# Cross-attention: where the first-pass matmuls of a block stand among its second-pass pairs

## What is computed

```python
q = qp.reshape(bsz, t, H, D).transpose(0, 2, 1, 3)      # H = 16, D = 32, t = 512
k = kp.reshape(bsz, s, H, D).transpose(0, 2, 1, 3)      # s = 8192
attn = jax.nn.softmax(jnp.einsum('bhtd,bhsd->bhts', q, k) * D ** (-0.5), axis=-1)
ctx = jnp.einsum('bhts,bhsd->bhtd', attn, v)
out = ctx.transpose(0, 2, 1, 3).reshape(bsz, t, H * D) @ out_w.T + out_b
```

## Time and profile before

| | |
|---|---|
| Time, median of 3 runs | 4093.96 us (4079.4 to 4094.05) |
| Profiled execution | 4091.75 us, of which the recorded span is 4090.4 us |
| PE busy | 3708.6 us, 91% of the span |
| DVE busy | 2603.6 us, 64% |
| POOL busy | 2185.1 us, 53% |
| ACT busy | 1871.6 us, 46% |
| Mean granted clock of PE | 0.936 |

### The profile page before, as it was taken

How to read it: one execution, slowest core, us unless ns; L and a number is a source line. 1 busy time by engine, 2 the same in 40 slices (tenths; PEclk the granted TensorE clock), 3 DMA queues, 4 the chain that set the end, 5 groups by cost and what they waited for, 6 DMA issues and landing times. The chain is left out here.

```text
span 4090.4 us, 46676 instructions
## 1 busy us (share of the span) xinstructions
PE 3708.6 (91%) x18156; PEld 2378.2 (58%) x18156; DVE 2603.6 (64%) x3405; ACT 1871.6 (46%) x1903; POOL 2185.1 (53%) x844
## 2 busy tenths in 40 slices
PE   8999999699999999875875999999998884999997
PEld 6888888455555555323663555555554483777775
DVE  3222222487777777365885877777774663888987
ACT  2111111245555555432553455555555221766664
POOL 0100110079999999532441599999996301555554
PEclk9999999789999999976897799999999896999998
DMA  7454544523233332004675133333320103888886
GB/s 254 155 173 154 176 160 160 163 70 88 74 88 81 91 83 73 1 22 155 270 278 159 52 86 81 91 83 83 91 69 13 47 1 126 314 316 336 326 332 229
DMA packets 194890, 572.78 MB, mean 140 GB/s; under 512 B 23888, under 2 KB 89456, under 8 KB 143088
## 3 DMA queue, kind: packets, MB, share of 16 engines
q1 hardware_dynamic: 155888, 496.39, 37.2%
q10 hardware_dynamic: 36864, 67.13, 4.3%
q0 software_dynamic: 1920, 6.29, 0.5%
HBM read 449.66 MB, written 120.06 MB: 139 GB/s over the span
## 5 line engine op out<-in xcount | busy, mean ns | idle before, releaser
L615 DVE TENSOR_REDUCE maxima<-psum 128x1 f32<-128x512 f32 x2048 | 1286.6, 683 | 393.4 <-PE psum L486 389.1
L583 ACT ACTIVATE pt<-psum 128x1024 f32<-128x1024 f32 x1024 | 1015.2, 1025 | 750.9 <-PE psum L494 745.6
L597 POOL TENSOR_TENSOR exp_sums<-pt 128x1024 f32<-128x1024 f32 x342 | 817.3, 2390 | 393.9 <-ACT pt L583 249.5
L486 PE MATMUL psum<-ks,first_q 96*128 96x512 f32 x2048 | 813.9, 457 | 42.5 <-DMA first_q<-q_parts 41.8
L600 POOL TENSOR_TENSOR exp_sums<-exp_sums,pt 128x1024 f32<-128x1024 f32 x310 | 736.9, 2377 | 44.5
L486 PEld LDWEIGHTS psum<-ks,first_q 96*128 96x128 f32 x2048 | 400.7, 196 | 487.1 <-DVE maxima L615 344.7
L506 PE MATMUL psum<-pt,vs 128*32 128x512 f32 x4096 | 674.3, 598 | 4.0 <-DVE head_rows L625 2.4
L1164 POOL TENSOR_TENSOR moe_cut<-moe_raw,moe_cut 128x2048 fp32r<-128x2048 f32 x84 | 444.1, 5287 | 425.5 <-ACT moe_cut L1247 425.3
L510 PE MATMUL psum<-exp_sums,constants 128*32 128x512 f32 x1408 | 670.1, 598 | 0.0
L494 PE MATMUL psum<-qs,ks 97*128 97x512 f32 x2048 | 647.4, 399 | 13.0 <-ACT pt L583 13.0
L1296 DVE TENSOR_TENSOR moe_cut<-moe_raw,moe_cut 128x2048 fp32r<-128x2048 f32 x160 | 535.1, 3355 | 87.4 <-ACT moe_cut L1247 87.4
(11 more groups left out here) (312 smaller groups left out, 4730.3 us busy)
## 6 DMA issues: line engine op xcount, KB each, us to landing
moe_raw<-in_moe_w SPq DMA_DIRECT2D x244, 1024.0 KB, 6.4
ks<-k_parts SPq DMA_DIRECT2D x384, 256.0 KB, 4.7
k_parts<-kparts ACTq DMA_DIRECT2D x256, 256.0 KB, 2.5
v_heads<-vrow SPq DMA_DIRECT2D x32, 1024.0 KB, 5.7
vs<-v_heads SPq DMA_DIRECT2D x32, 1024.0 KB, 5.3
cx<-in_ctx SPq DMA_DIRECT2D x16, 1024.0 KB, 9.0
first_q<-q_parts SPq DMA_DIRECT2D x96, 64.0 KB, 4.0
qs<-q_parts SPq DMA_DIRECT2D x96, 64.0 KB, 4.8
```

The lines of the kernel that those rows point to most:

```text
L486: pe.matmul(bank[b], self.first_q[s][:, t * P:(t + 1) * P], ks[s][0:3 * DH, keys:keys + CHUNK], start=True, stop=True).then_inc(*self.firs ...
L583: act.activation(self.pt[:, self.slot(h, b) + i:self.slot(h, b) + i + 2, :], self.c.psum[:, at:at + 2, :], ACT.Exp).then_inc(*self.exp.up())
L597: engine.tensor_tensor(to, self.pt[:, slot:slot + R, :], self.pt[:, slot + R:slot + 2 * R, :], ALU.add).then_inc(*signal.up())
L615: dve.tensor_reduce(self.maxima[:, h % 2, i % TT, i // TT:i // TT + 1], bank[b], X, ALU.max).then_inc(*self.first_read.up())
```

## The change

The loop in `head` takes 2, 1 and 2 first slots ahead of the three pairs of a block, and what is left, one slot, behind the last pair. DVE, ACT and POOL keep their orders; no instruction is added or removed.

```diff
@@ -306,6 +306,7 @@
     AHEAD = 12
+    FIRSTS = (2, 1, 2)
     RING = (LAG + 1) * BLOCK
@@ -526,12 +527,11 @@
                 todo = todo[:len(todo) - len(row)]
-                for i in range(0, len(tiles), 2):
-                    if todo:
-                        first_slot(todo.pop(0))
+                for i, ahead in zip(range(0, len(tiles), 2), self.FIRSTS):
+                    for k in todo[:ahead]:
+                        first_slot(k)
+                    todo = todo[ahead:]
                     second_pair(h, tiles[i])
-                    if todo:
-                        first_slot(todo.pop(0))
                     if i == 2 and b == self.LAG and h:
                         finish_head(h - 1)
                 for k in todo:
```

## The result

| | before | after |
|---|---|---|
| Median | 4094.2 us (4079.4 to 4101.86, 6 runs) | 4130.02 us (4125.09 to 4135.39, 6 runs) |
| Profiled execution | 4091.75 us, span 4090.4 us | 4130.96 us, span 4129.7 us |
| Mean granted clock of PE | 0.936 | 0.937 |

The ratio is 1.0093, with a 95% interval from 1.0079 to 1.0107: 0.93% slower, beyond the 0.5% that can be told from no change. The forecast was 4129 us and +0.86%.

The account below looks back on a forecast made before the run. PE was taken as the bound, busy throughout, with one 0.11 us wait for DVE per full block. +26.4 + 0.5 + 9.0 = +35.9 us on 4091.75 gave 4127.7, stated as 4129 us; range 4103 to 4146 us.

Parts of the forecast that it names:

- the second rival: Full blocks: the DVE wait's 0.11 us is gained and ACT does not hold the third pair; 4074 us, chance 0.06.
- Step 1: Full block: the second first slot, moved ahead of the first pair, removes the fifth's DVE wait, gaining 0.11 us.
- Step 2: Full block: the first pair, one matmul later, makes the third pair wait for ACT; net +0.10 us a block.
- the two bounds, 0 and 0.235 us: Full block's cost: 0 if the third pair's waiting load costs nothing extra, +0.235 us if the first pair's delay comes through whole.
- the rival built on it: Third pair's load is ready with the exponential, full blocks cost nothing, only finish_head's +9 us remains; 4103 us, chance 0.09.
- Step 3: Counting blocks: 264 full blocks in both layers at 0.10 us, +26.4 us; blocks with four first slots and three pairs, +0.5.
- Step 4: Block 2: finish_head now precedes the fourth first slot, delaying DVE and the weighing by 0.32 us; 28 times, +9.0 us.
- POOL's own 4.87: POOL's own period for its additions in a block, 2.54 + 2.33 = 4.87 us; a longer block gives it more room.

Follow-up runs that it names:

- new order, split exponentials: Changed slot order with finish_head left behind the fourth first slot, each 128x1024 exponential made as two of 128x512, against the kernel before: 4060.8 us, ratio 0.9917.
- new order, short exponentials: The changed kernel with ACT taking 384 of each bank's 512 columns per exponential, compared with the kernel before: 4070.0 us, ratio 0.9949.
- old order, short reading: The kernel before with DVE taking the maximum of 256 of 512 scores for heads 1 to 15, compared with the kernel before: 4049.4 us, ratio 0.9892.

## Why the prediction was right

**The reading of the block.** P2's 0.015 us to spare against ACT, worked out from rounded rows, is 0.061 - 0.051 = 0.010 us by the records: a load that has to wait for ACT comes 0.051 us after the exponential's end in the kernels where it waits. But this is the margin before P2's *load* moves, and not before the block pays, so the forecast did not turn on it, though the prediction says so. Five kernels show the difference (P2's load as the mean of 262 blocks, counted from the block's first load; the block as the plain one):

| kernel | P2's load | held by | full block |
|---|---|---|---|
| new order, split exponentials | 1.989 us | nothing | 4.864 us |
| new order, short exponentials | 2.103 us | ACT | 4.865 us |
| new order (after) | 2.315 us | ACT | 5.066 us |
| old order (before) | 2.092 us | F4's load, which waits for DVE | 4.962 us |
| old order, short reading | 2.084 us | ACT | 4.848 us |

Where nothing waits, the load is made while the matmul before it runs, 0.23 us ahead of its own matmul; one that waited has its matmul 0.10 us behind it. About 0.13 us of lateness are therefore swallowed: in the new order the load was 0.114 us late for nothing, and 0.326 us late for 0.202. F4 in the old order is the same case, 0.241 us late (1.984 us of the block against 1.743 with the short reading) for 0.114. The prediction's sum has this in it, since it counts P2's end from the row of head 15 (load and 0.73 us). Two of its sentences do not: that PE stands for about 0.33 us, which is the weight load's standstill and not the matmuls' 0.20, and the second rival's condition of some 0.33 us at P2, where an exponential 0.21 us shorter was enough.

**Step 1.** F4's wait did go: F3 and F4 take 0.64 us, and F4's load comes at 1.880 us of the block, where 1205.23 - 1203.35 = 1.88 was said. The short reading prices the wait at 0.114 us, where 0.11 was said.

**Step 2.** P2's load was foretold for 0.22 us later than before in the block (1205.67 against 1205.45), and came at 2.315 instead of 2.092 us, 0.223. A full block grew by 0.104, foretold 0.10. That is between the two bounds, 0 and 0.235 us: the load was not made ahead of its wait. The Trainium skill's rule on pulled loads, "TensorE: Matmul & The Clock Gate", section "Part 2: What happens when you issue a matmul", does not reach a load whose own semaphore is still out; P2's load and matmul start together in the rows of after, and the rival built on it (4103 us) falls.

**Step 3.** The count held: 262 full blocks can be followed in the records, the other two lie in the opening of each layer. +27.1 us against +26.4; the blocks with 4 slots +0.4 against +0.5.

**Step 4.** +0.320 us in 28 blocks, +9.0 us, as foretold; shown alone by the kernel with `finish_head` moved only.

**POOL.** It did not pace anything. In the kernel with short readings in the old order the full block went down to 4.848 us, under POOL's own 4.87, and stayed there. 4.87 us, which the expectation for that run allowed for as a floor, is thus none over a head: a head's last block gives POOL only one addition, by which it can catch up.

**What was not foreseen** is the clock in head 15, 1.2 us a layer. For the profiled execution 4127.7 us were worked out and 4130.96 measured, and most of these 3.3 us are it. That forecast and median lie 1 us apart is in part luck: the median was put 2.2 us above the profiled execution and lay 0.9 us below it. The fall does not go with the order of slots: in block 2 of head 15 it stands in the traces of after (both layers), of `finish_head` alone (one layer, 7.28 us), of both kernels with split exponentials and of short exponentials in the new order (one layer each), and in none of the other six. Without it that block takes 5.63 to 5.64 us where the exponentials are whole.

## What to carry to other kernels

Where two engines answer PE through rings of buffers, list for each wait how long before it the answer was there, and how late the waiting load can come before its matmul is late, here about 0.13 us. Moving work forward for the one moves it back for the other: F1 one matmul earlier gave back DVE's 0.11 us, P0 one matmul later cost 0.20. What helped both was a shorter round trip, here by signalling half as much at a time. And when a loop's shape is changed, what hangs on a place in it (here `finish_head` after the second pair) moves too: a quarter of the loss was that.

## What the runs showed of the hardware

- From the end of an exponential to the weight load that waits for it 0.049 to 0.052 us pass, and as much, 0.052 to 0.054, from DVE's L625 to the weighing's load where that waits for it.
- A weight load that waited has its matmul 0.10 us behind it; one that did not is made while the matmul before it runs, 0.23 us ahead of its own. So the first 0.13 us or so of a load's lateness cost nothing: 0.114 us late cost 0.001 us a block, 0.241 cost 0.114, and 0.326 cost 0.202.
- Three exponentials of 128x1024 as six of 128x512 cost ACT 0.17 us more in a block of the new order (2.87 to 3.04 us), though each half is recorded 0.61 us long: a queued exponential starts about 0.1 us before the last has ended, whole or half.
- PE's granted clock fell to 0.50 for some 3.4 us behind a stretch in which PE was busy 2.64 of 3.80 us, and stayed at 1.00 behind one of 2.62 of 3.80 us with the same instructions. No run here says why it falls only at times.
